# A two-layer graph network: carried segments merged in one go, with two scans for the maxima and a chain of products for the sums

## The reference, cut to what matters

```python
m = jax.ops.segment_max(score, col_idx, num_segments=n)
ex = jnp.exp(score - m[col_idx])
denom = jax.ops.segment_sum(ex, col_idx, num_segments=n)
alpha = ex / denom[col_idx]
agg = jax.ops.segment_sum(alpha[..., None] * msg_edge, col_idx, num_segments=n)
```

## Time and profile before

| | us |
|---|---|
| median of 3 runs (8269.59 to 8273.54) | 8271.29 |
| the profiled execution | 8273.5 |
| its span in the trace | 8271.8 |

### The profile page before, as it was taken

How to read it: one execution, slowest core, us unless ns; L and a number is a source line. 1 busy time by engine, 2 the same in 40 slices (tenths; PEclk the granted TensorE clock), 3 DMA queues, 4 the chain that set the end, 5 groups by cost and what they waited for, 6 DMA issues and landing times. The chain is left out here.

```text
span 8271.8 us, 122585 instructions
## 1 busy us (share of the span) xinstructions
PE 5780.7 (70%) x31102; PEld 4434.8 (54%) x31103; DVE 4736.4 (57%) x11348; ACT 3572.6 (43%) x9149; POOL 3624.3 (44%) x3761
## 2 busy tenths in 40 slices
PE   2999688788777752699465655555534564499999
PEld 2555465555555541488444444444423444288888
DVE  5555688888888864522433334444429997433333
ACT  0554577777777750112111111111107998133333
POOL 1221677777777741501477777777750000000000
PEclk7999899999999985889656665555558988599999
DMA  6554788888888861512311111122232222200000
GB/s 145 205 212 196 230 258 259 259 259 260 258 258 259 259 186 47 176 42 70 100 26 26 26 26 37 45 45 45 47 50 76 79 80 63 93 13 13 13 12 10
DMA packets 487748, 984.74 MB, mean 119 GB/s; under 512 B 116003, under 2 KB 275273, under 8 KB 480612
## 3 DMA queue, kind: packets, MB, share of 16 engines
q0 software_dynamic: 216416, 661.87, 26.6%
q1 hardware_dynamic: 247406, 298.35, 12.2%
q10 hardware_dynamic: 23680, 21.44, 0.8%
HBM read 785.43 MB, written 203.65 MB: 120 GB/s over the span
## 5 line engine op out<-in xcount | busy, mean ns | idle before, releaser
L1065 POOL DMA_INDIRECT ae_kv<-edge_table,ae_index x1664 | 1629.5, 979 | 525.7 <-issue 470.3
L2119 POOL DMA_INDIRECT g_row<-y,g_index x1664 | 1599.3, 961 | 527.9 <-issue 506.5
L2138 PE MATMUL psum<-g_row,g_hot 128*128 128x64 f32 x3328 | 670.8, 386 | 833.3 <-issue 765.1
L2138 PEld LDWEIGHTS psum<-g_row,g_hot 128*128 128x128 f32 x3328 | 650.1, 298 | 872.3 <-issue 789.2
L1283 PE MATMUL psum<-ae_kv,ae_edge_hot 128*128 128x266 f32 x3328 | 859.4, 402 | 330.1 <-DVE ae_kv L1144 294.3
L1283 PEld LDWEIGHTS psum<-ae_kv,ae_edge_hot 128*128 128x128 f32 x3328 | 601.8, 190 | 580.4 <-issue 377.1
L1252 PE MATMUL psum<-ae_q,ae_node_hot 128*128 x3328 | 781.3, 388 | 67.4 <-ACT ae_node_hot L1232 36.0
L1252 PEld LDWEIGHTS psum<-ae_q,ae_node_hot 128*128 128x128 f32 x3328 | 621.1, 192 | 166.8 <-issue 88.1
L2944 ACT ACTIVATE em_h<-psum,em_affine 128x256 f32<-128x256 f32 x800 | 408.6, 561 | 625.8 <-PE psum L2896 441.6
L2299 DVE TENSOR_TENSOR g_acc<-g_acc,g_step_sums 128x64 f32 x832 | 188.7, 227 | 719.2 <-ACT g_step_sums L2215 490.2
L1108 DVE TENSOR_TENSOR ae_kv<-ae_kv,psum 128x2048 f32<-128x2048 f32 x208 | 475.8, 2287 | 208.3 <-DMA ae_kv<-edge_table,ae_index 204.5
(11 more groups left out here) (545 smaller groups left out, 11248.4 us busy)
## 6 DMA issues: line engine op xcount, KB each, us to landing
ae_node_hot<-rel_rows SPq DMA_DIRECT2D x208, 512.0 KB, 5.6
gn_row<-source_places SPq DMA_DIRECT2D x208, 256.0 KB, 3.3
ae_kv<-edge_table,ae_index POOLq DMA_INDIRECT x1664
g_row<-y,g_index POOLq DMA_INDIRECT x1664, 2.4
x_sorted<-nt_x SPq DMA_DIRECT2D x52, 128.0 KB, 2.0
xt_kept<-nt_xt SPq DMA_DIRECT2D x52, 128.0 KB, 2.1
aa_xr<-x_sorted SPq DMA_DIRECT2D x52, 128.0 KB, 2.5
aa_xs<-xt_kept SPq DMA_DIRECT2D x52, 128.0 KB, 3.3
```

Source lines behind the costliest of these rows:

```text
L1065: g.indirect_dma_start(out=kv[:, s, n, :], out_offset=None, in_=dram["table"], in_offset=bass.IndirectOffsetOnAxis(ap=index[:, s, n:n + 1] ...
L2119: g.indirect_dma_start(out=row[:, m, n, :], out_offset=None, in_=table, in_offset=bass.IndirectOffsetOnAxis(ap=index[:, m, n:n + 1].bitcas ...
L2138: ins = t.matmul(bank[m][:, n // 2 * W:(n // 2 + 1) * W], hot[:, m, n, :], row[:, m, n, :], start=n % 2 == 0, stop=n % 2 == 1)
```

## The change: what it does

`merge_carried` is written anew, without a loop over blocks:

- All 1664 rows, keys and the keys of the next row (`keyn`) are loaded at the start, the rows in three parts (`CUTS`: blocks 0 to 3, 4 to 7 and 8 to 12). The keys go along the free axis of 4 partitions (`key4`) and of 128 (`keyr`).
- `index_tables` stores 128 more keys (zeros) behind the 1664, so that `keyn` can be read with an offset of one; `keys` is that much longer.
- The maxima of a key over all blocks are found by a scan forwards and a scan backwards over [4, 1664], with -1e30 added wherever the key changes; 13 transposes go there and 13 back.
- The sums go by one product for each block (`eq`), to which a second product is added that brings the total of the row before from the last block (`chain_hot` times `tot`). ScalarE copies each total out of PSUM before the next block's second product.
- Only the last row of a key in all 1664 writes its node. So no scatter's result is read again in the stage, and the 13 gathers and 13 scatters wait for no landing of each other.
- What VectorE does with the node rows is done for all blocks at once, and the last part in three pieces by `CUTS`.

The diff, cut: the first lines are in `index_tables`, the rest in `merge_carried`, whose removed loop stands above and is shown by its main waits alone.

```diff
-            sp.dma_start(dram["keys"].rearrange("(b p) -> p b", p=P), key[:], allow_slow_non_contiguous=True).then_inc(stored, 16)
+            sp.dma_start(dram["keys"][0:T].rearrange("(b p) -> p b", p=P), key[:], allow_slow_non_contiguous=True).then_inc(stored, 16)
+            sp.dma_start(dram["keys"][T:T + P].unsqueeze(0), c["zero"][0:1, 0:P]).then_inc(stored, 16)
 ...
-            sp.wait_ge(stored, 16 * (9 + RB))
+            sp.wait_ge(stored, 16 * (10 + RB))
 ...
-            with sp.Fori(0, RB) as b:
-                sp.wait_ge(merged, b)
-...
-                g.wait_ge(indexed, b + 1)
-                g.wait_ge(scattered, b * 16)
-...
-                v.wait_ge(scattered, b * 16)
-...
+        rows, node, tot = sbt("rows", [P, RB, CW]), sbt("node", [P, RB, CW]), sbt("tot", [P, RB, CW])
+        keyc, keyn, keyr = sbt("keyc", [P, RB]), sbt("keyn", [P, RB]), sbt("keyr", [P, T])
+        key4, ends = sbt("key4", [H, T]), sbt("ends", [H, T + 1])
+        fwd, mx = sbt("fwd", [H, T]), sbt("max", [H, T])
+...
+        CUTS = (0, 4, 8, RB)
+        rows_in = [sem(f"mc_rows_in{n}") for n in range(3)]
+...
+        def heads(x, a, b):
+            return x[:, a:b, C_V:CW].rearrange("p b (h d) -> p b h d", h=H)
+
+        def over_heads(x, a, b):
+            return x[:, a:b].unsqueeze(3).broadcast_to([P, b - a, H, DK])
+
+            sp.dma_start(keyc[:], dram["keys"][0:T].rearrange("(b p) -> p b", p=P), allow_slow_non_contiguous=True).then_inc(keys_in, 16)
+            sp.dma_start(key4[:], dram["keys"][0:T].unsqueeze(0).broadcast_to([H, T])).then_inc(four_in, 16)
+            for n in range(3):
+                a, b = CUTS[n], CUTS[n + 1]
+                sp.dma_start(rows[:, a:b], dram["carry"][a * P:b * P, :].rearrange("(b p) n -> p b n", p=P)).then_inc(rows_in[n], 16)
+            sp.dma_start(keyn[:], dram["keys"][1:T + 1].rearrange("(b p) -> p b", p=P), allow_slow_non_contiguous=True).then_inc(next_in, 16)
+            sp.dma_start(keyr[:], dram["keys"][0:T].unsqueeze(0).broadcast_to([P, T])).then_inc(spread_in, 16)
+            g.wait_ge(indexed, 1)
+            for b in range(RB):
+                g.indirect_dma_start(out=node[:, b, :], out_offset=None, in_=dram["sums"],
+                                     in_offset=bass.IndirectOffsetOnAxis(ap=gi[:, b:b + 1].bitcast(U32), axis=0)).then_inc(node_in, 16)
+            for n in range(3):
+                g.wait_ge(merged, n + 1)
+                for b in range(CUTS[n], CUTS[n + 1]):
+                    g.indirect_dma_start(out=dram["sums"], in_=node[:, b, :], in_offset=None,
+                                         out_offset=bass.IndirectOffsetOnAxis(ap=si[:, b:b + 1].bitcast(U32), axis=0),
+                                         bounds_check=TOP, oob_is_err=False).then_inc(scattered, 16)
+
+        @block.scalar
+        def _(a):
+            a.wait_ge(dw_ready, 1)
+            a.activation(w[:], dw[:], ACT.Exp).then_inc(w_ready, 1)
+            a.wait_ge(dab_ready, 2)
+            a.activation(ab[:], dab[:], ACT.Exp).then_inc(ab_ready, 1)
+            for b in range(RB):
+                a.wait_ge(added, b + 1)
+                a.activation(tot[:, b, :], bank[5 + b % 2][:, 0:CW], ACT.Copy).then_inc(kept, 1)
+            v.wait_ge(keys_in, 16)
+            ch.done(v.tensor_scalar(final_p[:], c["pcol"][:], float(P - 1), None, ALU.is_equal))
+            ch.link(v.tensor_scalar(valid[:], keyc[:], 0.0, None, ALU.is_ge))
+            ch.link(v.scalar_tensor_tensor(gi_f[:], keyc[:], float(-TOP), valid[:], ALU.add, ALU.mult))
+            v.tensor_scalar(gi[:], gi_f[:], float(TOP), None, ALU.add).then_inc(indexed, 1)
+            v.wait_ge(four_in, 16)
+            ch.done(v.memset(ends[:, 0:1], NEG))
+            ch.done(v.memset(ends[:, T:T + 1], NEG))
+            ch.link(v.tensor_tensor(ends[:, 1:T], key4[:, 1:T], key4[:, 0:T - 1], ALU.not_equal))
+            ch.done(v.tensor_scalar(ends[:, 1:T], ends[:, 1:T], NEG, None, ALU.mult))
+            for n in range(3):
+                a, b = CUTS[n], CUTS[n + 1]
+                v.wait_ge(rows_in[n], 16)
+                ch.link(v.tensor_scalar(off[:, a:b], rows[:, a:b, C_LAST], -1.0, -NEG, ALU.add, ALU.mult))
+                v.tensor_tensor(meff[:, a:b], rows[:, a:b, C_M:C_EX], off[:, a:b].unsqueeze(2).broadcast_to([P, b - a, H]), ALU.add
+                                ).then_inc(m_ready, 1)
+
+            v.wait_ge(next_in, 16)
+            ch.done(v.tensor_scalar(si_f[:], valid[:], -BIG, BIG, ALU.mult, ALU.add))
+            ch.link(v.tensor_tensor(more[:], keyc[:], keyn[:], ALU.is_equal))
+            ch.link(v.scalar_tensor_tensor(si_f[:], more[:], BIG, si_f[:], ALU.mult, ALU.max))
+            ch.link(v.tensor_tensor(si_f[:], si_f[:], keyc[:], ALU.add))
+            ch.done(v.tensor_scalar(si[:], si_f[:], 0.0, None, ALU.max))
+            ch.done(v.tensor_scalar(before[:], keyc[:], 7.0, final_p[:], ALU.add, ALU.mult))
+            ch.settle()
+            ch.link(v.tensor_scalar(before[:], before[:], -7.0, None, ALU.add))
+            v.wait_ge(m_turned, RB)
+            all4 = psum[0:H].rearrange("p b n -> p (b n)")[:, 0:T]
+            ch.link(v.tensor_tensor_scan(fwd[:], ends[:, 0:T], all4, NEG, ALU.add, ALU.max))
+            v.tensor_tensor_scan(mx[:, ::-1], ends[:, 1:T + 1][:, ::-1], fwd[:, ::-1], NEG, ALU.add, ALU.max).then_inc(swept, 1)
+            v.wait_ge(spread_in, 16)
+            for b in range(RB):
+                r = keyr[:, b * P:(b + 1) * P]
+                ins = v.tensor_scalar(eq[:, b, :], r, keyc[:, b:b + 1], None, ALU.is_equal)
+                if b:
+                    ch.done(ins)
+                    ins = v.tensor_scalar(chain_hot[:, b, :], r, before[:, b - 1:b], None, ALU.is_equal)
+                ins.then_inc(hots_ready, 1)
+            v.wait_ge(m_back, 1)
+            ch.link(v.tensor_copy(ms[:].rearrange("p b h -> p (b h)"), bank[4][:, 0:RB * H]))
+            v.tensor_tensor(dw[:], meff[:], ms[:], ALU.subtract).then_inc(dw_ready, 1)
+            v.wait_ge(w_ready, 1)
+            for n in range(3):
+                a, b = CUTS[n], CUTS[n + 1]
+                ch.link(v.tensor_tensor(rows[:, a:b, C_EX:C_V], rows[:, a:b, C_EX:C_V], w[:, a:b], ALU.mult))
+                v.tensor_tensor(heads(rows, a, b), heads(rows, a, b), over_heads(w, a, b), ALU.mult).then_inc(scaled, 1)
+            v.wait_ge(node_in, RB * 16)
+            ch.link(v.tensor_scalar(off_n[:], node[:, :, C_LAST], -1.0, -NEG, ALU.add, ALU.mult))
+            ch.link(v.tensor_tensor(mm[:], node[:, :, C_M:C_EX], off_n[:].unsqueeze(2).broadcast_to([P, RB, H]), ALU.add))
+            ch.link(v.tensor_tensor(mn[:], mm[:], ms[:], ALU.max))
+            v.tensor_tensor(dab[:, 0], mm[:], mn[:], ALU.subtract).then_inc(dab_ready, 1)
+            v.tensor_tensor(dab[:, 1], ms[:], mn[:], ALU.subtract).then_inc(dab_ready, 1)
+            v.wait_ge(ab_ready, 1)
+            for n in range(3):
+                a, b = CUTS[n], CUTS[n + 1]
+                ch.done(v.tensor_tensor(heads(node, a, b), heads(node, a, b), over_heads(ab[:, 0], a, b), ALU.mult))
+                ch.done(v.tensor_tensor(node[:, a:b, C_EX:C_V], node[:, a:b, C_EX:C_V], ab[:, 0, a:b], ALU.mult))
+                v.wait_ge(kept, b)
+                ch.done(v.tensor_tensor(heads(rows, a, b), heads(tot, a, b), over_heads(ab[:, 1], a, b), ALU.mult))
+                ch.done(v.tensor_tensor(rows[:, a:b, C_EX:C_V], tot[:, a:b, C_EX:C_V], ab[:, 1, a:b], ALU.mult))
+                ch.done(v.tensor_tensor(node[:, a:b, C_CNT], node[:, a:b, C_CNT], tot[:, a:b, C_CNT], ALU.add))
+                ch.settle()
+                v.tensor_tensor(node[:, a:b, C_EX:CW], node[:, a:b, C_EX:CW], rows[:, a:b, C_EX:CW], ALU.add).then_inc(merged, 1)
+            for b in range(RB):
+                n = sum(b >= x for x in CUTS[1:3])
+                t.wait_ge(m_ready, n + 1)
+                t.transpose(bank[b // 4][0:H, b % 4 * P:(b % 4 + 1) * P], meff[:, b, :], c["ident"][:]).then_inc(m_turned, 1)
+            t.wait_ge(swept, 1)
+            for b in range(RB):
+                ins = t.transpose(bank[4][:, b * H:(b + 1) * H], mx[:, b * P:(b + 1) * P], c["ident"][0:H, 0:H])
+            ins.then_inc(m_back, 1)
+            for b in range(RB):
+                n = sum(b >= x for x in CUTS[1:3])
+                t.wait_ge(hots_ready, b + 1)
+                t.wait_ge(scaled, n + 1)
+                wait_count(t, kept, b - 1)
+                ins = t.matmul(bank[5 + b % 2][:, 0:CW], eq[:, b, :], rows[:, b, :], start=True, stop=b == 0)
+                if b:
+                    t.wait_ge(kept, b)
+                    ins = t.matmul(bank[5 + b % 2][:, 0:CW], chain_hot[:, b, :], tot[:, b - 1, :], start=False, stop=True)
+                ins.then_inc(added, 1)
+
```

118 lines of the change are left out of this document (17 added, 101 removed).

## The result

| | before | after |
|---|---|---|
| median of 4 runs each, us | 8272.38 (8269.59 to 8273.54) | 8133.69 (8131.11 to 8134.87) |
| the profiled execution, us | 8273.5 | 8131.1 |
| the stage `merge_carried` in it, us | 203.8 | 63.2 |

The ratio of the times is 0.9832, with a 95% interval of 0.9815 to 0.9849; 138.7 us less by the medians. The forecast was 8135.

A forecast was written before the change was run, and what follows sets the result against it. No engine was at its limit; one serial chain of latencies cost the merge stage 203.8 us. The new path summed to 67.1, 136.7 less: 8273.5 became 8136.8, less 2.2 for the median, rounded to 8135; range 8124 to 8160.

The forecast's parts named there:

- first copy starts: ScalarE's first copy of a total, held behind the second exponential by instruction order: 33.0 us into the stage.
- the sum: Latencies added along the new merge stage's path, from keys to the next stage's first transfer: 67.1 us instead of 203.8.
- The chain: Twelve steps of second product and copy: 14.4 us all warm, 22.2 all cold, middle 18.3 taken.
- The end: After the last total: VectorE done at 55.1, last five scatters from 56.0, the eight before over by 53, next stage 67.1.
- The first rival: GpSimd is held up, all gathers at 2.55 us: +12.5, 8147 us; 8155 if the last five scatters too; chance 10%.
- 7 us of slack: Gathered node rows expected at 24.7 us into the stage, VectorE needing them only after the second exponential's preparation.
- the lock: VectorE and GpSimd share ports exclusively, delaying GpSimd's transfer descriptors; few operations of the new stage would ask for it.
- Slow pieces: Rival: the two piecewise key loads on the path are slow, 8214 us at 27 ns a piece, about 8160 at 15 us each; 8%.
- slower than before: Rival: all 4-byte pieces run on one of 16 transfer engines, 8338 us; it decides from 43 ns a piece; chance 2%.
- Gathers that aren't independent: Rival: each gather and scatter waits for the last landing, 4.7 us each, next stage at 138, total 8205 us; chance 3%.
- the zero for it: Cost of the extra row stored in `index_tables`: at most 0.5 us, taken as 0.
- a change of over 2 us elsewhere: Sign against the prediction: any stage other than the merge changing by more than 2 us.

The follow-up runs named there:

- 7: The kernel after, with ScalarE copying the first two totals before the second exponential: stage 59.4 us, where the kernel after took 63.2.
- 10: The kernel after, with twelve idle TensorE products ahead of the first block's, to raise its clock: stage 61.0 us, 2.2 shorter.
- 9: The kernel after, with VectorE's last part and the scatters in five pieces instead of three: stage 60.4 us, 2.8 shorter.
- 12: The kernel after, with the second scan also running forwards over two SBUF inputs (maxima then wrong): stage 61.8 us.
- 6: The kernel after, with the first scan writing to PSUM, so the second, backward scan reads one input from there: stage 63.4 us.
- 8: The kernel after, with the 1664 keys loaded once more into their own buffer ahead of `keyc`: stage 64.3 us, 1.1 longer.
- 5: The kernel after, with every gather and every scatter made to wait for the landing of the one before: stage 110.4 us, 47.2 longer.
- 1: The kernel before, with the loops of `merge_carried` written out: 8266.83 us beside 8264.91, stage 201.9.
- 4: The kernel before, written out, all rows and keys loaded first, and VectorE waiting only for the scatter two blocks back: 8225.61 us, stage 153.3.
- 11: The kernel after with the edits of 6, 7, 9 and 10 together: 9134.81 us against 9265.25 of the kernel before, ratio 0.9851, stage 58.2.

## Why the prediction was right, step by step

| t in us from the stage's start | predicted | measured |
|---|---|---|
| first reader of `keyc` | 4.0 | 3.05 |
| first, last gather starts | 5.5, 20.8 | 3.97, 24.6 |
| last third of the rows masked | 11 | 9.5 |
| scans start, end | 13.8, 21.1 | 11.1, 18.3 |
| comparisons end | 26.1 | 23.5 |
| first copy starts | 33.0 | 29.8 |
| last copy ends (12 steps) | 51.7 (18.3) | 46.4 (16.2) |
| VectorE's last addition ends | 55.1 | 49.6 |
| last five scatters from | 56.0 | 52.1 |
| last scatter starts | 61.3 | 57.25 |
| next stage | 67.1 | 63.2 |

**The order was the predicted one up to VectorE's last addition.** Keys, rows, two scans, comparisons, weights, second exponential, chain: each ended by what the sum had before it. 7 and 10 show from outside that the order of ScalarE and the clock stood on the path. But only as far as the chain's fourth total does this order set the stage's end (below). The durations read off smaller operations held: 3.6 for a scan (3.61), 1.22 and 1.49 for scaling four and five blocks (1.22, 1.49), 0.39 for a copy.

**Where the sum was off.** It was 3.9 us too long. Up to the first copy 3.2 went, 2.7 of it before the scans (11.1 instead of 13.8): the keys came 0.95 sooner, the last third of the rows 1.5, and `keyn`, which I had 1.6 behind the rows, was waited for by nobody. The chain took 16.2 instead of the middle of 14.4 and 22.2 that I had chosen: it was cold (1.77, estimated 1.85) for three steps alone and after one step of 1.36 warm (1.20, estimated 1.2). In the working the terms of a cold step add up to 1.81 (1.25 + 0.17 + 0.39) and not to 1.85, and those of the end to 55.0 and not to 55.1; together they change the forecast by less than 0.4.

**The end was another one.** I had the last five scatters wait for VectorE (55.1, then 56.0), and the eight before them over by 53, with 3 us to spare. VectorE was done at 49.6, and the eight weren't: held by operations of two inputs they took 13.1 us (3132.48 to 3145.59) instead of 8 x 1.33 = 10.6. By VectorE alone the last five would have gone at 50.5, 1.6 sooner. 5.5 us gained before, 1.6 lost at POOL, and 3.9 are left. So the path left the predicted one at the fourth total (t = 35.5): from there it went by VectorE's first piece to the first scatter (39.0), then through all 13 scatters (18.3 from the first's start to the last's), and 5.9 to the next stage. Of the twelve steps that the sum counted three lay on it. Of this the sum had nothing; 7, 9 and 12 show it, where the stage follows the row of scatters.

**The number itself came nearer than the mechanism.** The stage was 3.9 us shorter than the sum. In the profiled execution the other stages took off 1.7 more (4.1 longer before it, 5.8 shorter behind it), hence 8131.1 where the sum said 8136.8. The median of the four runs lies 2.6 above that execution. That 8133.69 stands 1.3 from 8135 is luck; what the reasoning can be held to is 63.2 against 67.1.

**The first rival came true in part, at a small price.** It had all gathers at 2.55 and 12.5 us lost. Three of 13 were held, at 3.00, 4.46 and 1.94; against 0.94 each that is 6.6 us, and the forecast had 7 us of slack there. Need and arrival met at 3122.0, by the estimate above. So this step was right by a narrow margin: one more hold of a scan's length would have been on the path. Of the scatters six were held (1.09 to 2.06), 2.8 us together, and of that come the 1.6 at POOL. I had written that few operations of the new stage would ask for the lock. That was wrong: the row at hand (2.55 beside 2.29) stood beside an operation with two inputs, and the new stage is full of those.
The Trainium skill ("SBUF — State Buffer", section "SBUF: two separate sides") says that an operation of VectorE in a 2-port mode, or one with two inputs in SBUF, takes the shared ports for the whole instruction, the latter only against a GpSimd operation that reads SBUF, and that whichever starts first gets them. If a gather or scatter counts as such a reader (its indices lie in SBUF; no run here tests it), the holds in 12 and beside the multiplications (2.06 beside 1.23) agree, and so do the free gathers beside the first scan (one input in PSUM) and the free scatter of 12 that started in time. In the hold in 6 one input lay in PSUM, so this rule doesn't give it.

**The other rivals.** Slow pieces fell by 8 (at most 0.8 ns; 43 were needed to be slower than before). Gathers that aren't independent would have been 5: 110.4, where the rival said 138; it had the scatters at 4.7 us each, and they take 3.38, the gathers 3.83. In the kernel after each gather but the first has "issue" before it and 0.30 us of idle time, so none waits for a landing.

**Elsewhere.** The added store takes SyncE 2.27 us, and the one behind it is held for less. Timeline of the first stage after, to be set against the 6.09 of the earlier trace rows:

```profile
116.48 2.27 SPq L210 DMA_DIRECT2D carry_keys<-zero  x1
118.79 3.19 SPq L211 DMA_DIRECT2D step_blocks<-blk_i  x1
```

2.27 + 3.19 is less than 6.09, and the next stage begins 1.4 sooner and not later, so the zero for it stands. I had written that a change of over 2 us elsewhere would prove me wrong; 4.1 and 5.8 were seen, of opposite sign, in stages of unchanged code. The bound was too tight for single profiled executions, whose total alone varies by 4 us between runs.

**Where the time came from.** Not from work removed alone: 2 us from the loop (1), 48.6 once landing and reload are both off VectorE's path (4), then from 153.3 to 110.4 with the small operations done once for 13 blocks, and from 110.4 to 63.2 by independent transfers (5). 4 and 5 aren't on one line of kernels, so the 42.9 between them is a difference and no experiment of its own; that the small operations are its cause is argued and not shown.

## What to carry to other kernels

Where a loop waits for two things that end near each other, the gain of removing either is small and that of removing both is large: 6.9 and 4.5 us singly, 48.6 together. Take dependent rounds apart by making their order unnecessary (here: only the last row of a key writes), and the transfers then cost their issue, 1.25 to 1.29 us each, and not their landing, 3.4 to 3.6. When a sum of latencies ends on one engine's row of transfers, count what holds that engine beside the others, and see how much slack each branch has left.

## What the runs showed of the hardware that was not expected

- An indirect transfer of GpSimd that starts beside a long two-input operation of VectorE ends 0.83 to 0.90 us after it, as if its own 0.94 us began only then: 4.46 and 3.59 us beside scans of 3.61, 1.94 beside 1.22, 2.06 beside 1.23. Only the first gather (3.00) ends later, 1.19 us after a comparison of 1.87 and 0.14 after the operation of one input behind it. The scan with its data in PSUM, forwards, held none in nine traces. The backward scan with one input in PSUM did (6, 11). A forward scan from SBUF held it too (12). What the backward scan from PSUM has to do with it stays open; a backward scan was not tried on its own.
- A transfer that has begun before the operation isn't held. In 5 and 7 a gather started 0.23 and 0.25 us ahead of the second scan and took 0.94 and 0.95, and the scan its 3.61 all the same. In 12 a scatter that started together with a multiplication took 1.01, where it took 2.06 when it started 0.05 behind.
- 1664 pieces of 4 bytes loaded to 128 partitions cost 0.9 to 1.3 us (8), while SyncE spent 4.34 us on the issue of one load of 852 KB (`keyr`) behind the other loads.
- The same kernel took 8272 us in one set of runs and 9276 in another. In the long stage of gathers a slice moves 256 to 261 GB/s where the total is near 8200 and 209 to 213 where it is near 9200; the merge stage is the same (63.2 and 63.4). In the slower surroundings the saving of 11 was 130 us in the total, where the stages' lengths (203.8 in the faster ones) differ by 145.6. It isn't the chip alone: 9 to 11 and 12 are on record for one and the same chip, and the kernel before took 9265 us there beside 9 to 11 and 8287 beside 12. What sets it stays open.
